# One of eight slots of each attention group read on TensorE from the table in SBUF, and the attention products in four column tiles

## The chip, the cores and the metric

The program runs on one core of one Trainium2 chip. The metric is the device time of one execution, in microseconds (us). PE is the matrix engine, DVE the vector engine, ACT the activation engine, POOL the engine that issues the gathers here, and SP issues the other DMAs.

## What is computed

A graph network on 3125 nodes (32 numbers each) and 100000 edges sorted by destination: an edge MLP, two graph convolutions and three attention layers with residuals and normalisations. The attention layer, where the change is, is this, with 8 heads of 32:

```
xl = (x @ Wl).reshape(-1, H, C); xr = (x @ Wr).reshape(-1, H, C)
e = leaky_relu(xl[src] + xr[dst], 0.2)
logits = einsum('ehc,hc->eh', e, att)
m = segment_max(logits, dst)
p = exp(logits - m[dst])
alpha = p / segment_sum(p, dst)[dst]
out = segment_sum(alpha[:, :, None] * xl[src], dst).mean(axis=1) + bias
```

## The kernel before

Edges stand in 832 slots of 128 edges. A group is 8 slots (104 groups), a chunk is 8 groups (13 chunks). The node rows lie in a table, in SBUF during a layer and in DRAM: per node 32 numbers in f32 and the same in three bf16 parts. Each attention layer goes once over the 104 groups.

For every group, POOL gathers the source rows with eight indirect DMAs (`pool_gathers`, L340), one for each slot, into one of two buffers, so it is at most two groups ahead. ACT copies the f32 part to `xs` (`keep`, L562). PE turns the source rows and reads the destination rows out of four windows (`rows_in`, L833 and L836: 48 matmuls of 128 columns, each in one of four 32-column tiles of the array), ACT copies the result (`turn`, L566), PE forms the 256 edge features in two halves (`z_half`, L848), ACT takes the relu (`leaky`, L573), and PE sums them to logits (`linear`, L856, and `logits_half`, L865, once for each half, in two column tiles). The logits of eight groups gather in one PSUM bank.

At a chunk's end (phases 0, 1 and 2 of the next chunk) DVE scans the logits for the maximum by destination (L1445, L1449). In phase 0 four transposes (L905) and `exchange` on one partition carry it over the pieces; in phase 1 `settle` subtracts it, ACT takes the exponential (L606) and PE turns the weights (L911); in phase 2 `fscale` follows a small product (L894) and scales one window of `acc`. Ten groups later (`LAG`) DVE multiplies `xs` by the weights (`weigh`, L1432, two halves), PE sums over edges (`sums_half`, L877, two halves of eight instructions), and DVE adds the sums to `acc` (`add`, L1442).

PE's order in step u, written out by hand, is: `z_half(u, 0)`, `sums_half(k, 0)`, `linear(u)`, `z_half(u, 1)`, `logits_half(u, 0)`, `rows_in(u + 1)`, `sums_half(k, 1)`, `logits_half(u, 1)`, with k = u - 10. DVE's is `weigh`, `add`, `weigh`, `add`. Semaphores join the engines, and each engine takes its instructions in this order.

Before each layer DVE makes the table, PE forms 25 windows of self logits (L947), DVE reads them (L1040, L1539), reduces them in one instruction (L1542), and clears `acc` (L1548). The convolutions already read some slots from the table in SBUF: DVE makes one-hot matrices with `is_equal` (L1304), PE multiplies them with the table (L761, 12 matmuls for one slot), DVE masks the result (L1309).

## Time and profile before

| | |
|---|---|
| median of 3 runs | 6472.8 us (6467.22 to 6487.99) |
| the profiled execution, its own time | 6470.45 us |
| its span, first to last instruction | 6468.7 us |
| PE, PE weight loads | 84%, 55% of the span |
| POOL, DVE, ACT | 65%, 50%, 30% |
| the chain that ended last | PE 40%, POOL 29%, issue 15%, DVE 9% |
| the three attention layers | from about 2734 us to 6468 us |

A line of the profile names the engine, the line of the program, the operation, what it writes and reads, and its count. "issue" is time in which the engine waited for nothing that the profile shows. Weight loads overlap the matmuls. An f32 matmul stands as two instructions. Matmuls are pipelined, so the step from one line's start to the next line's start, not the duration, is what a group of them costs.

### The profile page before, as it was taken

What the parts mean: (1) busy time and instruction counts of PE and PEld (TensorE: products, weight loads), DVE (VectorE), ACT (ScalarE), POOL (GpSimd) and SP (SyncE); (2) the same over time, 40 slices, a digit from 0 to 9 for tenths busy, and PEclk for the clock granted to TensorE, in tenths of its full rate; (3) what the DMA queues carried; (4) which work ended last, traced back from release to release, by engine and by line L of the source; (5) the groups of instructions that cost most, each with busy time, mean ns of one, the idle gap of its engine ahead of it and who ended that gap; (6) DMA issues with size and microseconds to landing.
All of it is one profiled execution on the core that took longest, in us unless ns stands there. A gap on an engine that the chain in (4) does not pass through costs nothing.

```text
span 6468.7 us, 138175 instructions
## 1 busy us (share of the span) xinstructions
PE 5462.8 (84%) x47565; PEld 3535.7 (55%) x47565; DVE 3216.3 (50%) x5767; ACT 1959.8 (30%) x3916; POOL 4227.3 (65%) x4383
## 2 busy tenths in 40 slices
PE   1888888868886888689999986899999679999995
PEld 1666666667775777535455544354444444455553
DVE  8222323266567555535555555355555624555555
ACT  0333334345551000033333321333333123333330
POOL 0777777657775777477777742777777147777770
PEclk8899989879997999789999996999999879999997
DMA  1444444323332332234444431444444224444441
GB/s 36 113 114 113 113 113 113 102 72 83 78 83 66 83 83 77 54 87 119 117 121 121 120 94 38 104 120 117 121 121 118 65 56 116 120 119 121 119 117 32
DMA packets 645340, 626.97 MB, mean 97 GB/s; under 512 B 366244, under 2 KB 447915, under 8 KB 644779
## 3 DMA queue, kind: packets, MB, share of 16 engines
q1 hardware_dynamic: 498218, 437.16, 22.1%
q0 software_dynamic: 140352, 181.29, 14.6%
q8 instruction: 312, 5.11, 0.3%
q10 hardware_dynamic: 6208, 1.37, 0.1%
q14 instruction: 250, 2.04, 0.1%
HBM read 530.77 MB, written 88.55 MB: 96 GB/s over the span
## 4 chain that ended last, share of the span: by engine, by line
PE 40%; POOL 29%; issue 15%; DVE 9%; ACT 2%; DMA 2%; DVEq 1%; POOLq 0%
POOL rows L340 29%; PE ps L761 11%; PE ps L877 10%; PE ps L848 4%; PE ps L776 4%; PE ps L865 2%; PE ps L856 2%; DMA rows<-table,idx 2%; DVE region L1326 1%; DVE acc L1442 1%; PE ps L947 1%; PE ps L833 1%; PE ps L788 1%; DVE region L1034 1%; PE ps L963 1%
## 5 line engine op out<-in xcount | busy, mean ns | idle before, releaser
L340 POOL DMA_INDIRECT rows<-table,idx x3328 | 3231.9, 971 | 1556.8 <-issue 1108.3
L877 PE MATMUL ps<-region,hot 128*128 128x272 f32 x4992 | 1320.0, 408 | 92.2 <-DVE acc L1442 87.9
L877 PEld LDWEIGHTS ps<-region,hot 128*128 128x128 f32 x4992 | 910.9, 192 | 507.9 <-issue 335.8
L573 ACT ACTIVATE region<-ps 128x512 f32<-128x512 f32 x1248 | 677.4, 595 | 1681.9 <-PE ps L848 1681.9
L1442 DVE TENSOR_TENSOR acc<-acc,ps 128x272 f32 x1248 | 545.2, 437 | 1195.6 <-PE ps L877 1088.5
L1432 DVE TENSOR_TENSOR region<-ps,region 128x1056 f32<-128x1056 f32 x624 | 781.7, 1253 | 64.8 <-issue 53.7
L761 PE MATMUL ps<-hot,region 128*128 128x192 bf16 (+1 forms) x7488 | 773.0, 266 | 13.2 <-issue 9.6
L848 PE MATMUL ps<-xT,wcat 64*128 64x512 f32 x2496 | 721.9, 655 | 7.4 <-ACT region L573 4.9
L761 PEld LDWEIGHTS ps<-hot,region 128*128 128x128 bf16 x7488 | 701.9, 105 | 40.8 <-issue 9.9
L352 POOL DMA_INDIRECT rows<-table,idx x528 | 502.6, 952 | 270.5 <-issue 160.3
L865 PE MATMUL ps<-region,attblk 128*32 128x512 f32 x2496 | 667.5, 614 | 0.0
L352 POOL DMA_INDIRECT region<-table,idx x512 | 487.2, 952 | 156.0 <-issue 156.0
L848 PEld LDWEIGHTS ps<-xT,wcat 64*128 64x128 f32 x2496 | 193.4, 189 | 463.8 <-issue 431.0
L1289 DVE TENSOR_TENSOR acc<-acc,ps 128x96 f32 (+1 forms) x832 | 252.2, 303 | 354.4 <-PE ps L788 127.5
L833 PEld LDWEIGHTS ps<-identb,rows 128*32 128x32 bf16 x7488 | 239.8, 97 | 270.5 <-issue 264.5
L833 PE MATMUL ps<-identb,rows 128*32 128x128 bf16 x7488 | 300.0, 223 | 93.1 <-DMA rows<-table,idx 89.4
L620 ACT ACTIVATE region<-iota,region 128x128 bf16<-128x128 f32 x832 | 254.2, 389 | 283.3 <-PE ps L796 270.9
L856 PE MATMUL ps<-xT,linblk 128*128 128x512 f32 x624 | 331.3, 613 | 0.0
L836 PE MATMUL ps<-turned,xwin 128*32 128x128 bf16 x7488 | 313.2, 223 | 0.0
L1231 DVE TENSOR_TENSOR region<-ps,b3row 128x512 f32<-128x512 f32 x104 | 71.9, 691 | 483.5 <-PE ps L725 483.5
L776 PE MATMUL ps<-region 128*128 128x224 f32 x1248 | 308.3, 371 | 0.0
L1309 DVE TENSOR_TENSOR region<-ps,gmask 128x448 f32<-128x448 f32 x312 | 193.8, 621 | 176.8 <-PE ps L761 176.0
(264 smaller groups left out, 5880.0 us busy)
## 6 DMA issues: line engine op xcount, KB each, us to landing
hot<-hot_dram SPq DMA_DIRECT2D x624, 256.0 KB
turned<-turned_dram SPq DMA_DIRECT2D x624, 128.0 KB
rows<-table,idx POOLq DMA_INDIRECT x3856
hot_dram<-hot SPq DMA_DIRECT2D x104, 512.0 KB
xwin<-table SPq DMA_DIRECT2D x1664, 24.0 KB
region<-hot_dram SPq DMA_DIRECT2D x78, 512.0 KB
turned_dram<-turned SPq DMA_DIRECT2D x104, 256.0 KB
region<-r_dram SPq DMA_DIRECT2D x78, 256.0 KB
```

Source lines behind the costliest of these rows:

```text
L340: pool.indirect_dma_start(rows[:, b, j, :], None, table, bass.IndirectOffsetOnAxis(ap=idx[:, s:s + 1], axis=0)).then_inc(gathered[b], 16)
L352: pool.indirect_dma_start(rows4[at % 4][:, j, :], None, table, bass.IndirectOffsetOnAxis(ap=idx[:, 8 * g + j:8 * g + j + 1], axis=0)).then ...
L573: act.activation(rz[:, 2 * t + side, :], ps[:, Z + side, :], ACT.Relu).then_inc(rz_made, 1)
L761: mm = pe.matmul(ps[:, GB + i % 2, 224 * j:224 * j + n], bt[b][:, k, at:at + P], tabparts[:, k::FOLD, (2 + s) * C:(3 + s) * C], start=(k = ...
L776: mm = pe.matmul(ps[:, DB[i % 2], 0:GROUPS * C], dhot[b][:, at, :], picked[b][:, at, :, :].rearrange("p g c -> p (g c)"), start=(j == 0), ...
L833: m1 = pe.matmul(ps[q:q + C, XT, j * P:(j + 1) * P], rowparts[b][:, at, 2 * C + s * C:2 * C + (s + 1) * C], identb[:, :], start=(s == 0), ...
L848: pe.matmul(ps[:, Z + side, :], wcat[l][q:q + 64, side, t * P:(t + 1) * P], xT[q:q + 64, g % 2, :], start=True, stop=True).then_inc(z_summ ...
L856: pe.matmul(ps[:, LG, :], linblk[l][:, (7 - n) * H:(7 - n) * H + P], xT[:, g % 2, :], start=(n == 0), stop=False, skip_group_check=True)
L865: pe.matmul(ps[q:q + 32, LG, :], attblk[l][:, t, p_:p_ + 4 * H], rz[:, 2 * t + side, :], start=False, stop=(n % 4 == 3 and t == 1), skip_g ...
L877: mm = pe.matmul(ps[:, AG + i, 0:PC + H], hot[:, b, 4 * side + 2 * i + j, :], px[b][:, 4 * side + 2 * i + j, :], start=(j == 0), stop=(j = ...
L1432: v.tensor_tensor(to, at.unsqueeze(3).broadcast_to([P, 4, H, HK]), xs[:, (k // 8) % 2, n, 4 * side:4 * side + 4, :].unsqueeze(2).broadcast ...
L1442: v.tensor_tensor(at, at, ps[:, AG + i, 0:PC + H], ALU.add).then_inc(att_added, 1)
```

## The change

In the attention layers the eighth slot of each group is no longer gathered: POOL issues seven indirect DMAs. In its place, two groups ahead, `read_one` multiplies a one-hot matrix with the table in SBUF (12 bf16 matmuls into the free columns of the first sum bank), and DVE's `pick_one` masks out the right 32 of 224 columns and sums them into `xs`. `rows_in` turns that slot with one f32 matmul in place of three bf16 ones, and waits for it. The one-hot matrices come once a chunk from four `is_equal` of 128x1024 (`stationary_one`), whose row numbers SP fetches with a broadcast DMA of 128 x 8 pieces of 256 bytes. A contiguous bf16 copy of the table (`tabC`) is made at each layer's start. There the reduction L1542 becomes seven smaller ones inside the loop over windows, and the first `pick_one` stands behind the clearing of `acc`.

The two `logits_half` become one `logits` at the end of the step: four products in four column tiles, where each half had two in two. For this the order of logits in the bank is changed from (piece, head) to (head, piece), with which the copies and views of `exchange`, `weigh`, `fall` and `fdiag` change, and two copies of `exchange` become four.

```diff
-                slots = range(8 * g, 8 * g + 8) if pas == 0 else piece_slots(g)
+                slots = range(8 * g, 8 * g + 8) if pas == 0 else piece_slots(g)[0:7]
...
+            def numbers_for(c):
...
+                if at >= 2:
+                    sp.wait_ge(bt1_made, FOLD * (at - 1))
+                first = CHUNK * c + CHUNK // 2 + PIECE - 1
+                sp.dma_start(rline1[at % 2].rearrange("p (n e) -> p n e", n=8),
+                             r_dram.rearrange("a (f e) -> (a f) e", f=2)[first:first + 29:4, :].partition_broadcast(P)
+                             ).then_inc(r1_in[at % 2], 16)
...
+                pe.wait_ge(one_kept, l * G + g + 1)
                 for j in range(4):
                     for s in range(3):
                         for side in range(2):
                             q, at = 64 * side, 4 * side + j
...
+                            elif s == 0:
+                                m3 = pe.matmul(ps[q:q + C, XT, j * P:(j + 1) * P], xs[:, (g // 8) % 2, g % 8, 7, 0:C],
+                                               ident[:, :], start=True, stop=True)
+                                m3.then_inc(x_made, 1)
...
-            def logits_half(g, t):
+            def logits(g):
                 n = g % 8
-                pe.wait_ge(rz_made, 4 * (l * G + g) + 2 * t + 2)
+                pe.wait_ge(rz_made, 4 * (l * G + g) + 4)
                 for side in range(2):
...
+                    for t in range(2):
+                        q = 64 * side + 32 * t
+                        pe.matmul(ps[q:q + 32, LG, :], attblk[l][:, t, 7 - n:7 - n + 32], rz[:, 2 * t + side, :],
+                                  start=False, stop=(n == 7), skip_group_check=True).then_inc(l_summed, 1)
+
+            def read_one(g):
...
+                for k in range(FOLD):
+                    cols = len(range(k, W, FOLD)) * C
+                    for s in range(3):
+                        mm = pe.matmul(ps[:, AG, 272:272 + cols], bt1[at % 2][:, k, n, :],
+                                       tabC[:, k::FOLD, s * C:(s + 1) * C], start=(k == 0 and s == 0),
+                                       stop=(k == FOLD - 1 and s == 2), skip_group_check=True)
+                mm.then_inc(one_read, 1)
...
+                if side == 1 or k + LAG + 2 >= G:
+                    pe.wait_ge(one_picked, l * G + min(k + LAG + 3, G))
...
+            read_one(0)
             rows_in(0)
+            read_one(1)
...
                 if u < G:
                     z_half(u, 0)
+                if u + 2 < G:
+                    if k > 0:
+                        pe.wait_ge(att_added, 4 * (l * G + k))
+                    read_one(u + 2)
...
-                    logits_half(u, 0)
...
-                    logits_half(u, 1)
+                    logits(u)
...
+            def pick_one(l, g):
...
+                v.tensor_tensor(cand, ps[:, AG, 272:272 + GROUPS * C].rearrange("p (g c) -> p g c", g=GROUPS),
+                                wide(spanhot[:, g, :], C), ALU.mult).then_inc(one_picked, 1)
+                v.wait_ge(one_picked, at + 1)
+                v.tensor_reduce(xs[:, (g // 8) % 2, g % 8, 7, 0:C], cand.rearrange("p g c -> p c g"), AX.X, ALU.add
+                                ).then_inc(one_kept, 1)
...
+                v.tensor_copy(tabC, tabparts[:, :, 2 * C:5 * C]).then_inc(tab_kept, 1)
+                attention_begins(l)
...
+                    if w % 4 == 3 or w == W - 1:
+                        lo = w - w % 4
+                        link(v.tensor_reduce(selfsum[:, lo:w + 1, :].rearrange("p w h -> p (w h)"),
+                                             prodself[:, 0:w + 1 - lo, :].rearrange("p w (h c) -> p (w h) c", h=H),
+                                             AX.X, ALU.add))
```

In DVE's step `pick_one(u + 2)` stands between `add(k, 0)` and the second `weigh`; in phases 3 and 4 two `stationary_one` each stand ahead of the first `weigh`. In `rows_in` the fourth slot of the second side is the one that is read.

## Rows read from the trace of the kernel before

**Rows 1.** Windows of 150 us inside the first attention layer: us, busy by engine, clock.
```profile
3300.00:3450.00 150.00, 146.76 (x1251) 75.33 (x1252) 79.96 (x127) 50.68 (x110) 112.41 (x118) 1.00 0.46 118
```
**Rows 2.** Timeline of POOL, first gathers: start, us, line, [idle before <- released by].
```profile
2740.07 0.94 POOL L340 DMA_INDIRECT rows<-table,idx  x1 [57.88 <-DMA table<-hot]
2741.32 0.94 POOL L340 DMA_INDIRECT rows<-table,idx  x1 [0.30 <-issue]
```
**Rows 3.** Line L856 (two per group): groups 0 to 10, then 10 to 103.
```profile
L856 PE MATMUL ps<-xT,linblk x22: 592/697/1222, 2769.1 to 2868.5; 128*128 128x512 f32 x22
...
L856 PE MATMUL ps<-xT,linblk x188: 592/593/697, 2868.1 to 3819.1; 128*128 128x512 f32 x188
```
**Rows 4.** Timeline of PE over one ordinary group, merged by line.
```profile
3302.80 2.10 PE L877 MATMUL ps<-region,hot 128*128 128x272 f32 x8
3304.83 1.05 PE L865 MATMUL ps<-region,attblk 128*32 128x512 f32 x4
3305.81 1.13 PE L848 MATMUL ps<-xT,wcat 64*128 64x512 f32 x4
3306.87 2.10 PE L877 MATMUL ps<-region,hot 128*128 128x272 f32 x8
3308.81 1.02 PE L856 MATMUL ps<-xT,linblk 128*128 128x512 f32 x2
3309.76 1.13 PE L848 MATMUL ps<-xT,wcat 64*128 64x512 f32 x4
3310.82 0.62 PE L865 MATMUL ps<-region,attblk 128*32 128x512 f32 x2
...
3312.47 2.10 PE L877 MATMUL ps<-region,hot 128*128 128x272 f32 x8
```
**Rows 5.** Timeline of PE in a convolution: the same table read, two slots.
```profile
1403.35 2.22 PE L761 MATMUL ps<-hot,region 128*128 128x224 bf16 x24
1405.41 0.95 PE L776 MATMUL ps<-region 128*128 128x224 f32 x4
```
**Rows 6.** Timeline of PE: the 48 transposes of one group by themselves, and what follows.
```profile
3260.00 0.23 PE L836 MATMUL ps<-turned,xwin 128*32 128x128 bf16 x1
...
3260.78 0.27 PE L905 MATMUL ps<-ident,region 128*1 128x128 f32 x1
```
**Rows 7.** Timeline of PE in the groups after a chunk's end.
```profile
3271.76 0.66 PE L911 MATMUL ps<-ident,region 128*128 128x128 f32 x4
...
3278.96 0.38 PE L894 MATMUL ps<-fdiag,ones 8*128 8x8 f32 x2
...
3283.48 2.07 PE L877 MATMUL ps<-region,hot 128*128 128x272 f32 x8 [0.35 <-DVE acc L1442]
```
**Rows 8.** Timeline of ACT in the same groups: the exponential.
```profile
3271.08 0.63 ACT L606 ACTIVATE region<-region 128x512 f32<-128x512 f32 x1
```
**Rows 9.** Timeline of DVE in the same groups.
```profile
3261.41 0.41 DVE L1043 COPY ahead<-ps 1x256 f32<-1x256 f32 x1 [1.94 <-PE ps L905]
...
3279.39 0.23 DVE L1037 TENSOR_SCALAR fscale<-ps,first_hot 128x8 f32<-128x8 f32 x1 [3.11 <-PE ps L894]
...
3282.90 0.44 DVE L1442 TENSOR_TENSOR acc<-acc,ps 128x272 f32 x1 [0.36 <-DVE acc L1442]
```
**Rows 10.** DVE by line and shape: count | busy us, mean ns | idle before.
```profile
L1304 DVE TENSOR_SCALAR region<-region,lanes 128x1024 bf16<-128x1024 f16 x312 | 158.1, 508 | 2.9
...
L1289 DVE TENSOR_TENSOR acc<-acc,ps 128x224 f32 x312 | 120.4, 386 | 108.5 <-PE ps L776 104.5 <-issue 1.0 <-DVE acc L1289 0.7
```
**Rows 11.** Timeline of DVE and PE at the first layer's start.
```profile
2764.71 6.81 DVE L1542 TENSOR_REDUCE hot<-region 128x200 f32<-128x6400 f32 x1
...
2773.51 5.72 DVE L1548 MEMSET acc<- 128x6800 f32 x1 [1.59 <-issue]
...
2764.85 0.29 PE L833 MATMUL ps<-identb,rows 128*32 128x128 bf16 x1 [0.72 <-DVE lself L1539]
```
**Rows 12.** The page's DMA issues: count, KB each, us from issue to landing.
```profile
table<-hot SPq DMA_DIRECT2D x6, 1000.0 KB, 5.8
```

More of the change, by code:

```diff
@@ L146, in build @@
         lane = sb("lane", [P, 1])
-        fall = sb("fall", [H, 1])
-        fdiag = sb("fdiag", [H, H])
+        fall = sb("fall", [8 * H, 1])
+        fdiag = sb("fdiag", [8 * H, H])
+        headsel = sb("headsel", [8 * H, H])
+        spanhot = sb("spanhot", [P, G, GROUPS], BF16)
         fscale = sb("fscale", [P, H])
@@ L276, in build @@
         r_made, r_stored = sem("r_made"), sem("r_stored")
+        r1_in = [sem(f"r1_in{b}") for b in range(2)]
+        bt1_made, one_read, one_picked, one_kept = sem("bt1_made"), sem("one_read"), sem("one_picked"), sem("one_kept")
+        tab_kept = sem("tab_kept")
         r_in = [sem(f"r_in{b}") for b in range(2)]
@@ L560, in keep @@
             def keep(g):
-                act.wait_ge(gathered[g % 2], 128 * ((1 + l) * HALF + g // 2 + 1))
-                act.activation(xs[:, (g // 8) % 2, g % 8, :, 0:C], rows[:, g % 2, :, 0:C], ACT.Copy).then_inc(xs_kept, 1)
+                act.wait_ge(gathered[g % 2], 128 * HALF + 112 * (l * HALF + g // 2 + 1))
+                act.activation(xs[:, (g // 8) % 2, g % 8, 0:7, 0:C], rows[:, g % 2, 0:7, 0:C], ACT.Copy).then_inc(xs_kept, 1)
             def turn(g):
@@ L893, in pe_attention @@
                     pe.wait_ge(endmax_copied, at + 1)
-                    pe.matmul(ps[:, MISC, 0:H], ones[0:H, :], fdiag[:, :], start=True, stop=True).then_inc(fall_spread, 1)
+                    pe.matmul(ps[:, MISC, 0:H], ones[0:8 * H, :], fdiag[:, :], start=True, stop=True).then_inc(fall_spread, 1)
                 if u < G:
@@ L1207, in _ @@
             cp(grp, slint)
+            ones_of = grp.rearrange("p (c a n j) -> p c a n j", c=CHUNKS, a=2, n=8)[:, :, 1, :, PIECE - 1]
+            for c in range(CHUNKS):
+                tt(spanhot[:, 8 * c:8 * c + 8, :], wide(ones_of[:, c, :], GROUPS), down(iota[:, 0:GROUPS], 8), ALU.is_equal)
             for k in range(FOLD):
@@ L1415, in _, with stationary_one, attention_begins @@
             cp(X0[:, :, :], X[:, :, :])
+            selfsum = T1[:, :, :].rearrange("p w c -> p (w c)")[:, 512:512 + W * H].rearrange("p (w h) -> p w h", w=W)
+            def stationary_one(l, c, k):
+                at = l * CHUNKS + c
+                if k == 0:
+                    v.wait_ge(r1_in[at % 2], 16 * (at // 2 + 1))
+                    if at >= 2:
+                        v.wait_ge(one_read, l * G + 8 * (c - 1))
+                v.tensor_scalar(bt1[at % 2][:, k, :, :].rearrange("p n e -> p (n e)"), rline1[at % 2], lanes[:, k:k + 1],
+                                None, ALU.is_equal).then_inc(bt1_made, 1)
+            def pick_one(l, g):
+                at = l * G + g
+                v.wait_ge(one_read, at + 1)
+                if at > 0:
+                    v.wait_ge(one_kept, at)
+                v.tensor_tensor(cand, ps[:, AG, 272:272 + GROUPS * C].rearrange("p (g c) -> p g c", g=GROUPS),
[3 more added lines that the diff above has]
+                                ).then_inc(one_kept, 1)
+            def attention_begins(l):
+                for k in range(FOLD):
+                    stationary_one(l, 0, k)
             def attention(l):
@@ L1455, in exchange @@
                     v.wait_ge(tails_turned, 4 * at + 4)
-                    got = ps[0:1, MISC, :].rearrange("p (s k r h) -> p s k h r", s=2, k=2, r=PIECES)
-                    cp(ahead[:, :, :, 1:PIECES + 1], got[:, 0, :, :, :])
-                    cp(behind[:, :, :, 0:PIECES], got[:, 1, :, :, :])
+                    got = ps[0:1, MISC, :].rearrange("p (s k a h n) -> p s a k h n", s=2, k=2, a=2, h=H)
+                    for a in range(2):
+                        cp(ahead[:, :, :, 1 + 8 * a:9 + 8 * a], got[:, 0, a, :, :, :])
+                        cp(behind[:, :, :, 8 * a:8 + 8 * a], got[:, 1, a, :, :, :])
                     lines = [t.rearrange("p h r -> p (h r)") for t in (ahead[:, 0, :, :], ahead[:, 1, :, :],
@@ L1482, in settle @@
                                            ALU.is_lt, ALU.mult).then_inc(lasts_made, 1)
-                    tt(fall[:, :], carrycol[0:H, 0:1], most_[0:H, 0:1], ALU.subtract)
-                    v.tensor_scalar(fall[:, :], fall[:, :], 0.0, first_old[0:H, c:c + 1], ALU.min, ALU.mult).then_inc(e_made, 1)
-                for u in range(8, G + LAG):
+                    tt(fall[:, :], carrycol[0:8 * H, 0:1], most_[0:8 * H, 0:1], ALU.subtract)
+                    v.tensor_scalar(fall[:, :], fall[:, :], 0.0, first_old[0:8 * H, c:c + 1], ALU.min, ALU.mult).then_inc(e_made, 1)
+                pick_one(l, 0)
+                pick_one(l, 1)
+                for u in range(G + LAG):
                     phase, c, k = u % 8, u // 8 - 1, u - LAG
@@ L1498, in attention, with pick @@
                         link(v.tensor_tensor(at, at, fscale[:, :].unsqueeze(2).broadcast_to([P, H, HK]), ALU.mult))
+                    def pick():
+                        if u + 2 < G:
+                            pick_one(l, u + 2)
+                    if phase in (3, 4) and u // 8 + 1 < CHUNKS:
+                        for q in range(2):
+                            stationary_one(l, u // 8 + 1, 2 * (phase - 3) + q)
                     if phase == 0 and ends:
@@ L1506, in attention @@
                             add(k, 0, windows)
+                        pick()
                         if 0 <= k + 1 < G:
@@ L1526, in attention @@
                             add(k, 0, windows)
+                        pick()
                         if 0 <= k + 1 < G:
```

81 lines of the change are left out of this document (49 added, 32 removed).

## The prediction

> **What bounds the kernel now.** I read the busy shares by window first. Inside an attention layer PE is busy 146.8 of 150 us at the full clock of 2.4 GHz (granted 1.00), DVE 80.0, ACT 50.7, POOL 112.4 [rows 1]. POOL's share misleads: between two gathers lie 0.30 us of issue, so one gather costs 1.25 us from start to start [rows 2], eight cost 10.0 and the 64 of a chunk 80.0. PE's ordinary group runs from L877 at 3302.80 to L877 at 3312.47, 9.67 us [rows 4]. The layer's pace, from the starts of L856 for groups 10 to 103, is (3819.1 - 0.4 - 2868.1) / 93 = 10.22 us, 81.8 a chunk (0.4 is the second instruction of the last pair) [rows 3]; the other two layers repeat it. So PE and the gathers are nearly level. A chunk is 8 x 9.67 = 77.4 of ordinary PE work, and the other 4.4 are work and waits at the chunk's end and waits for gathered rows. Two pieces are otherwise bound: in the first ten groups no edge sums run yet, and they take 99 us, the gathers' ten times 10.0 [rows 3]; at a layer's start PE waits for DVE [rows 11].
>
> **The change part by part: one group on PE.** The steps between starts [rows 4] are: z_half 1.06 twice, first sums 1.94, linear 0.95, logits_half with rows_in 1.65, second sums 2.04, last logits_half 0.98.
>
> Added: read_one is twelve matmuls. In the convolution 24 of them take 2.06 (1403.35 to 1405.41) [rows 5], so 1.03. It is in the same full-array tiling as the sums behind it, so no new switch.
>
> Removed: rows_in alone takes 0.78 [rows 6], so the first logits_half had 1.65 - 0.78 = 0.87 of the step. The last one stays at 0.98 if its eight instructions in four column tiles run together as its four in two tiles do. That is not shown for f32. The nearest row is rows_in itself, 48 matmuls of 128 columns in 0.78, which is four tiles streaming at once (48 x 128 columns at 2.4 GHz one after another would be 2.56 us). I take 0.98; the other end is one pair after the other, 0.87 more.
>
> Changed: rows_in has an f32 matmul for three bf16 ones. By its twelve per tile the pitch is about 0.06; f32 takes four passes for three, so 0.83 (between 0.78 and 1.0).
>
> Sum: 1.06 + 1.03 + 1.94 + 0.95 + 1.06 + 0.83 + 2.04 + 0.98 = 9.89, or 0.22 more than 9.67, and 1.8 a chunk.
>
> **The chunk's end.** Phase 1: the weights' transposes (L911, 3271.76) start as ACT's exponential ends (3271.08 + 0.63 = 3271.71) [rows 7, 8]; the exponential stands behind the relu of the second z_half, which doesn't move. What hid it was a logits_half and rows_in. With the first logits_half gone PE arrives 0.82 earlier and waits: 0.8 is given back.
>
> Phase 2: the second sums (3283.48) start as the second add ends (3282.90 + 0.44) [rows 7, 9], after the chain L894 (3278.96), fscale (3279.39), scaling, weigh, add. The sums now also wait for the multiply of pick_one behind that add. Its nearest row is a DVE operation of 224 columns with a PSUM operand, 0.39 [rows 10]. PE arrives 0.82 earlier, the release comes 0.33 later: 1.15. Queued behind PE's wait are the sums, the logits and all of the next group. In ordinary groups the pick has nearly 3 us of linear, z_half and rows_in as cover and costs nothing; if that cover failed it would be up to 0.9 a group.
>
> Phase 0: exchange copies 256 numbers of one partition in 0.41 [rows 9], twice; halves in four copies I estimate at 0.29 each, 0.3 more on the path to the carry (bounds 0 and 0.8). The four is_equal of 0.51 [rows 10] a chunk fall in phases 3 and 4, where DVE has idle time: 0.
>
> **The other waits.** read_one waits for the adds of the group before, a wait that the first sums had and that now comes 1.03 earlier; in ordinary groups logits and z_half, 2.04 [rows 4], lie between the sums and it, and an add is 0.44 [rows 9], so 0. Behind it stand both sums. rows_in waits for the pick of the step before: 0. SP's queue gets one more DMA a chunk and a wait for is_equal made a chunk earlier; behind it stand the loads of windows and of one-hot matrices, which run two groups ahead: 0, and at most the DMA's own time, 5.8 [rows 12], once a chunk if that lead were gone.
>
> **The gathers.** Seven cost 8.75 a group, 70 a chunk, and wait for nothing that PE then waits for. What PE waits for them now is between 0 and 81.8 - 80.0 = 1.8 a chunk; I take back 1.0. So a gain of 10 us on POOL is worth 1 us here, because PE's order is next at once.
>
> Per chunk: 1.8 + 0.8 + 1.15 + 0.3 - 1.0 = +3.05. Times 93 / 8 = 11.6 chunks and three layers: +106 us.
>
> **The first ten groups** follow the gathers: nine groups at 1.25 less are -11.2; PE's chain at the first chunk's end (scan, exchange, settle) holds some back, so -9, three times: -27 (bounds -34 and -15).
>
> **A layer's start.** rows_in(0) started at 2764.85, released by DVE's last read of a window [rows 11]. Now it needs pick_one(0), which stands behind the clearing of acc. First, DVE must have its row numbers before the windows: their DMA goes out once the table has landed (2740.07 is that landing [rows 2]), 256 KB in 1024 pieces, at least a fraction of, at most about, the 5.8 of the table's 1000 KB [rows 12]; then four is_equal, 2.0 [rows 10]. Some of that DVE had idle; I take a delay of 4 (0 to 8). The seven reductions hold the loop 1 longer. Behind it come a last small reduction and an add, 0.8; then what stands now between the add's end (2764.71 + 6.81 + 0.4) and the end of L1548 (2773.51 + 5.72), 7.3 [rows 11]; then pick_one, 0.9. Together 14, three times: +42 (bounds 27 and 57). The old reduction of 6.81 was behind PE's start and is worth nothing there. POOL's third group waits for rows_in(0), so it moves too.
>
> **Before the layers** DVE makes 13 comparisons and splits 8 flag copies into 16, all on one chain: between 0.2 and 0.39 each [rows 10], +4. No cover.
>
> Sum: 106 - 27 + 42 + 4 = +125. Against the profiled execution's 6470.45 that is 6595; that execution is 2.4 us under the median, so nothing is corrected for.
>
> On the four tiles a rule of the skill speaks against the count. The Trainium skill, "TensorE: Matmul & The Clock Gate", section "Measured speedup vs the span model", gives 2.38 times for three column tiles and 3.07 times for four row tiles of 512 columns. By 3.07 the logits would take an estimated 1.11 where I take 0.98, and the sum would be 41 us more. No row of this trace has four f32 tiles.
>
> **The rivals.** (1) The column tiles do not run together in f32: the array takes one pair, then the other, and the removed logits_half comes back behind the second sums, where it covers none of the new waits: 0.87 x 312 = +271, 6866. For: no row shows four f32 streams. Against: four bf16 streams run [rows 6].
>
> (2) No new waits: DVE and ACT shift ahead with PE so the 0.8 and 1.15 vanish, and the DMA of row numbers is covered. Then -1.95 x 34.9 = -68 and -12: 6515. For: idle time of DVE. Against: in both places PE starts within 0.15 us of the end of the work that releases it [rows 7 to 9].
>
> (3) Faster: the layer really follows gathers. Mechanism: most of the chunk's 4.4 us above 77.4 are late gathers and their echo in the waits at the chunk's end. Its place is rows_in; its price is the share that goes. Rival 2's chunk is 81.8 + 2.1 - 1.0; it decides from the point where more than 2.1 of the 4.4 are gathers' doing. With 3.4 of them gone a chunk is 1.3 shorter, -45; with -34 in the first groups, +30 at the starts and +4: 6425. For: POOL is 29% of the chain that ended last, and PE and POOL are level. Against: 81.8 - 80.0 bounds the share at 1.8, unless echoes count.
>
> (4) The pick is late in ordinary groups too (0.3 or more a group): 6690 and up.
>
> **How the numbers follow.** Forecast 0.60 (6545 to 6650 by the bounds of its terms), (1) 0.09, (2) 0.14, (3) 0.08, (4) 0.09. The range is 6480 to 6710: it takes in (2), the forecast and the lower half of (4), and leaves out (1) and (3). Within 0.3% (19 us, about what a measurement of this kernel can tell from no change) is the lower end of (2) and the upper of (3), 0.09; faster by more 0.07; slower by more 0.84.
>
> **What would show it.** The step from L856 to the next in ordinary groups: 9.9, not 9.67. The logits: 0.98 to 1.1 for eight instructions; 1.85 is rival 1. A wait of 1 us before the weights' transposes and of 1.6 before the second sums of phase 2; none there is rival 2. PE's waits for gathered rows gone inside a layer, and gaps of POOL of 1 us and more for every group. rows_in(0) some 39 us after the table's landing in place of 25. The first ten groups in about 90. The prediction is wrong if the ordinary step is under 9.7, or if the waits at the chunk's end were the gathers' echo.

## The result, and the profile after

The changed kernel takes 6550.64 us (median of 4 runs, 6542.4 to 6556.77), the kernel before on the same chip 6470.52 (4 runs): ratio 1.0117, 95% interval 1.0096 to 1.0139. It is slower, by 80 us (1.2%); forecast were 6595 and a range of 6480 to 6710. The profiled execution has 6542.4 us of its own, a span of 6540.7 and a granted clock of 0.924. The two profiled executions differ by 72 us, and the readings below add up to that.

The window of [rows 1] (us, busy by engine, clock):

```profile
3300.00:3450.00 150.00, 146.33 (x1358) 84.28 (x1350) 92.22 (x158) 47.49 (x105) 97.63 (x103) 1.00 0.47 122
```

The line of the linear product (two instructions a group) over the two stretches of [rows 3]:

```profile
L888 PE MATMUL ps<-xT,linblk x22: 592/607/1114, 2782.9 to 2873.5; 128*128 128x512 f32 x22
...
L888 PE MATMUL ps<-xT,linblk x188: 592/592/697, 2873.0 to 3846.5; 128*128 128x512 f32 x188
```

The timeline of POOL at its first gather in the layers, beside [rows 2]:

```profile
2741.29 0.94 POOL L350 DMA_INDIRECT rows<-table,idx  x1 [58.09 <-DMA table<-hot]
```

PE is as full as it was (146.3 of 150 us at full clock, before 146.8), DVE has 12 us more, POOL 15 less. The first ten groups take 90.1 us in place of 99.0 [rows 3]; from there the pace is (3846.5 - 0.4 - 2873.0) / 93 = 10.46 us a group in place of 10.22.

One ordinary group on PE, merged by line, beside [rows 4] (start, us, line, shapes):

```profile
3327.29 2.10 PE L926 MATMUL ps<-region,hot 128*128 128x272 f32 x8
3329.32 1.06 PE L897 MATMUL ps<-region,attblk 128*32 128x512 f32 x8
3330.32 1.13 PE L880 MATMUL ps<-xT,wcat 64*128 64x512 f32 x4
3331.38 1.21 PE L910 MATMUL ps<-region 128*128 128x224 bf16 x12
3332.42 2.03 PE L926 MATMUL ps<-region,hot 128*128 128x272 f32 x8
3334.29 1.02 PE L888 MATMUL ps<-xT,linblk 128*128 128x512 f32 x2
3335.24 1.13 PE L880 MATMUL ps<-xT,wcat 64*128 64x512 f32 x4
...
3337.13 2.10 PE L926 MATMUL ps<-region,hot 128*128 128x272 f32 x8
```

The step is 3337.13 - 3327.29 = 9.84 (9.67 before). By starts: sums 2.03, the eight logits 1.00 (L897), z_half 1.06, the read 1.04 (L910), sums 1.87, linear 0.95, and 1.89 for z_half with rows_in.

The timeline of PE in the groups at a chunk's end, beside [rows 7]:

```profile
3360.53 0.28 PE L975 MATMUL ps<-ident,staterow 1*128 1x1 f32 x2 [0.31 <-DVEq L1560]
3362.20 1.21 PE L910 MATMUL ps<-region 128*128 128x224 bf16 x12 [0.33 <-DVE acc L1530]
3368.91 0.66 PE L966 MATMUL ps<-ident,region 128*128 128x128 f32 x4 [0.90 <-ACT region L631]
3381.80 2.07 PE L926 MATMUL ps<-region,hot 128*128 128x272 f32 x8 [1.49 <-DVE region L1495]
```

The timeline of DVE in the same groups, beside [rows 9]:

```profile
3357.43 0.28 DVE L1098 COPY ahead<-ps 1x128 f32<-1x128 f32 x1 [0.53 <-PE ps L960]
3381.27 0.38 DVE L1495 TENSOR_TENSOR region<-ps,spanhot 128x224 f32<-128x224 f32 x1
```

And that of ACT, beside [rows 8]:

```profile
3368.23 0.63 ACT L631 ACTIVATE region<-region 128x512 f32<-128x512 f32 x1
```

Two waits of PE are new in size: 0.90 before the weights' transposes, ended by ACT's exponential, and 1.49 before the second sums, ended by the first instruction of `pick_one` (L1495). Before they were 0.05 and 0.35. The third, 0.33 before the read for DVE's add, only moved: before, the first sums of this group waited for that add, in the same timeline of the kernel before:

```profile
3266.05 2.07 PE L877 MATMUL ps<-region,hot 128*128 128x272 f32 x8 [0.41 <-DVE acc L1442]
```

The timeline of DVE at the first layer's start, beside [rows 11]:

```profile
2744.46 1.70 DVE L1486 TENSOR_SCALAR region<-T,lanes 128x1024 bf16<-128x1024 f16 x4 [7.62 <-DMA T<-r_dram]
2769.93 5.72 DVE L1653 MEMSET acc<- 128x6800 f32 x1 [1.62 <-issue]
2776.04 0.39 DVE L1495 TENSOR_TENSOR region<-ps,spanhot 128x224 f32<-128x224 f32 x1
```

And PE's rows_in(0):

```profile
2777.14 0.27 PE L860 MATMUL ps<-identb,rows 128*32 128x128 bf16 x1 [7.32 <-DVE region L1498]
```

rows_in(0) starts at 2777.14 where it started at 2764.85, and the 7.32 us ahead of it are a wait for the pick behind the clearing of `acc`.

The waits between 3000 and 3800 us (us in total, times, longest):

```profile
POOL rows L350 <- ACT region L587: 137.5, 66, 4.7
PE ps L926 <- DVE region L1495: 13.8, 9, 1.8
PE ps L966 <- ACT region L631: 9.0, 10, 0.9
```

POOL now has idle time in nearly every group (66 waits, 2.1 us on average); PE waits for the pick once a chunk and in no ordinary group.

Where the 72 us are, from the starts of the linear product and of rows_in in all three layers:

| stretch | forecast | measured |
|---|---|---|
| up to the first table store | +4 | +1.2 |
| three layer starts | +42 | +36.7 |
| three times groups 0 to 10 | -27 | -21.7 |
| three times groups 10 to 103 | +106 | +57.3 |
| the rest | 0 | -1.5 |

The first four experiments ran on one chip, with the kernel before at 6471.23 us (one of its 13 executions there took 21197.4 us and is left out of the ratios); that is within 1 us of the 6470.52 beside the changed kernel, so their times are set beside its 6550.64. The others ran on two further chips, on which the kernel before itself took 8225.59 and 8211.69 us, so their ratios to it are what can be compared; where two times are given, they are from these two chips in this order. The changed kernel itself was run on neither.

### The profile page after: what moved, and what is told of

The parts are those of the page before. It is cut to its first block, busy times and chain, and to the rows that moved or that the text cites. A ratio compares the mean times of both kernels' runs of the same rounds, so it can differ in the third digit from the quotient of the medians.

```text
span 6540.7 us, 146855 instructions
## 1 busy us (share of the span) xinstructions
PE 5464.1 (84%) x50997; PEld 3747.4 (57%) x50997; DVE 3552.2 (54%) x6668; ACT 1937.5 (30%) x3916; POOL 3931.6 (60%) x4071
## 4 chain that ended last, share of the span: by engine, by line
PE 61%; POOL 15%; DVE 10%; issue 10%; ACT 2%; DVEq 1%; DMA 1%; POOLq 0%
PE ps L926 18%; POOL rows L350 15%; PE ps L786 11%; PE ps L880 8%; PE ps L910 5%; PE ps L897 4%; PE ps L801 4%; PE ps L888 3%; PE ps L860 2%; DVE region L1386 1%; PE ps L813 1%; DVE acc L1530 1%; DVE region L1089 1%; PE ps L1018 1%; ACT region L598 1%
## 5 line engine op out<-in xcount | busy, mean ns | idle before, releaser
L350 POOL DMA_INDIRECT rows<-table,idx x3016 | 2936.8, 974 | 1927.3 <-issue 962.5
L926 PE MATMUL ps<-region,hot 128*128 128x272 f32 x4992 | 1299.1, 404 | 114.5 <-DVE region L1495 49.7
L362 POOL DMA_INDIRECT rows<-table,idx x528 | 502.8, 952 | 264.6 <-issue 160.3
L910 PEld LDWEIGHTS ps<-region 128*128 128x128 bf16 x3744 | 310.4, 99 | 262.3 <-issue 213.3
L910 PE MATMUL ps<-region 128*128 128x192 bf16 (+1 forms) x3744 | 382.6, 253 | 18.1 <-DVE acc L1530 12.2
L860 PEld LDWEIGHTS ps<-identb,rows 128*32 128x32 bf16 x6552 | 212.8, 97 | 300.8 <-issue 300.8
L897 PE MATMUL ps<-region,attblk 128*32 128x512 f32 x2496 | 343.5, 621 | 2.6 <-ACT region L598 2.6
L860 PE MATMUL ps<-identb,rows 128*32 128x128 bf16 x6552 | 267.5, 222 | 64.7 <-DMA rows<-table,idx 42.7
```

The lines of the kernel that those rows point to most:

```text
L350: pool.indirect_dma_start(rows[:, b, j, :], None, table, bass.IndirectOffsetOnAxis(ap=idx[:, s:s + 1], axis=0)).then_inc(gathered[b], 16)
L362: pool.indirect_dma_start(rows4[at % 4][:, j, :], None, table, bass.IndirectOffsetOnAxis(ap=idx[:, 8 * g + j:8 * g + j + 1], axis=0)).then ...
L860: m1 = pe.matmul(ps[q:q + C, XT, j * P:(j + 1) * P], rowparts[b][:, at, 2 * C + s * C:2 * C + (s + 1) * C], identb[:, :], start=(s == 0), ...
L897: pe.matmul(ps[q:q + 32, LG, :], attblk[l][:, t, 7 - n:7 - n + 32], rz[:, 2 * t + side, :], start=False, stop=(n == 7), skip_group_check=T ...
L910: mm = pe.matmul(ps[:, AG, 272:272 + cols], bt1[at % 2][:, k, n, :], tabC[:, k::FOLD, s * C:(s + 1) * C], start=(k == 0 and s == 0), stop= ...
L926: mm = pe.matmul(ps[:, AG + i, 0:PC + H], hot[:, b, 4 * side + 2 * i + j, :], px[b][:, 4 * side + 2 * i + j, :], start=(j == 0), stop=(j = ...
```

## The experiments

The theory going in: PE's order binds the changed kernel; the chunk's two waits (exponential, pick) and the pick behind the clearing are what it lost beyond the ordinary step; the four tiles run together. The main rival: the gathers still matter, in the kernel before above all.

### The four tiles alone

The kernel before with the new logits, all eight gathers and no read.

```diff
-                    logits_half(u, 0)
...
-                    logits_half(u, 1)
+                    logits(u)
```

> The kernel before with the second half of the change alone: all eight slots are gathered, none is read from the table, and the four logits products of a group stand at the end of the step in four column tiles (with the new order of logits in the bank). Theory (PE's order sets the pace, the gathers stand just behind it): PE's ordinary group falls from 9.67 to 8.8 us, but eight gathers stay at 10.0, so the group goes to 10.0, the chunk from 82.0 to about 81, and the layers' starts stay as they were: about 6440 us, 0.3 to 0.7 per cent faster than before. Rival (waits for gathers are small and PE's work is what counts): each chunk is 5 us or more shorter, 6290 us. Rival (four f32 column tiles cost as much as two pairs): no gain, 6470 to 6500 us.

Measured: 6465.72 us (10 runs), ratio 0.9997, interval 0.9987 to 1.0007. No change. Its groups 10 to 103 of the first layer, by the line of the linear product:

```profile
L885 PE MATMUL ps<-xT,linblk x188: 592/592/698, 2871.7 to 3825.1; 128*128 128x512 f32 x188
```

Its waits between 3000 and 3800 us (us in total, times, longest):

```profile
POOL rows L350 <- issue: 193.7, 597, 2.5
POOL rows L350 <- ACT region L586: 8.5, 28, 0.3
PE ps L858 <- DMA rows<-table,idx: 49.8, 41, 2.8
```

The same waits in the kernel before:

```profile
POOL rows L340 <- issue: 198.8, 610, 3.5
POOL rows L340 <- ACT region L562: 4.9, 16, 0.3
PE ps L833 <- DMA rows<-table,idx: 6.9, 16, 1.3
```

PE's unobstructed group is 8.82 us here, 0.85 under the 9.67 of before, so it is not the rival of four tiles that cost as much as two pairs, though the time alone would fit that too. The pace is (3825.1 - 0.4 - 2871.7) / 93 = 10.25. The 0.85 went into waiting: for gathered rows the profile names 49.8 us in 800 where it named 6.9. The gathers are the reason. In both kernels POOL's mean distance from gather to gather in that window is 1.28 us, not the 1.25 of two neighbours [rows 2], and 8 x 1.28 = 10.24, the pace of both. By itself that equation says nothing, since any steady loop with eight gathers has an eighth of its pace as their mean distance. What decides is that POOL hardly waits: for a free buffer 4.9 us of 800 before and 8.5 here. The mean is 1.28 also over the second to eighth gather of every group alone, before which the program has no wait. Most of what lifts it over 1.25 is one distance of 3.0 to 4.5 us that comes in the attention layers at nearly every 112th gather (21 of 22 times in the kernel before), always the second of a group. One of them in POOL's timeline of the kernel before:

```profile
3321.67 0.94 POOL L340 DMA_INDIRECT rows<-table,idx  x1 [2.23 <-issue]
```

So the kernel before did not have the gathers near its bound: it ran at their pace. What the 112 comes from, no run shows.

### The read alone

The changed kernel with the logits back in two halves of two tiles each, at their old places.

```diff
+                    logits_half(u, 0)
                 if u + 1 < G:
                     rows_in(u + 1)
...
-                    logits(u)
+                    logits_half(u, 1)
```

> The changed kernel with the logits back in two halves at their old places, two column tiles each: the read from the table alone. Theory: PE's ordinary group is 9.83 + 0.87 = 10.7 us, 7.0 a chunk; the half ahead of rows_in covers the wait for the exponential (0.9) and part of the wait for the pick in phase 2 (0.9 of 1.5) again, so a chunk is 84.0 + 7.0 - 1.7 = 89.3 and the time 6542 + 35 x 5.3 = about 6728 us. Rival (the waits at the chunk's end are not a matter of cover): they stay, 6542 + 35 x 7.0 = 6787 us. Rival (the four tiles save less than a half): under 6680 us.

Measured: 6723.41 us, ratio 1.0382 (1.0364 to 1.0401), as the theory had it. PE in an ordinary group:

```profile
3327.97 1.05 PE L896 MATMUL ps<-region,attblk 128*32 128x512 f32 x4
3328.95 1.13 PE L880 MATMUL ps<-xT,wcat 64*128 64x512 f32 x4
```

Four instructions in two tiles take 0.98 here, eight in four tiles 1.00 in the changed kernel. The pace is 11.09 us a group. The four tiles are thus worth 6723 - 6551 = 172 us beside the read and 0 without it: the same edit, with PE's order as the bound in the one kernel and the gathers in the other.

### The exponential ahead of the relus

In phase 1 ACT takes the exponential before the relu of the second z_half, not behind it.

```diff
-                if u < G:
-                    leaky(u, 1)
                 if phase == 1 and 0 <= done < CHUNKS:
                     act.wait_ge(d_made, l * CHUNKS + done + 1)
                     act.activation(weight, weight, ACT.Exp).then_inc(weight_made, 1)
+                if u < G:
+                    leaky(u, 1)
```

> The changed kernel with one swap on ACT: in phase 1 the exponential of the weights stands ahead of the relu of the second half. Theory: PE's wait of 0.90 before the transposes of the weights goes, but the second sums behind them then wait for the pick (its multiply ends at 3368.70, the sums start at 3369.41), so 0.6 a chunk are won: -21 us, 6521 to 6530 us. Rival (that wait is an echo of DVE's chain and comes back elsewhere): no change, 6550 us. Rival (nothing is next): -31 us.

Measured: 6524.08 us, ratio 1.0076 (1.0058 to 1.0094); 26 us under the changed kernel. The line of the weights' transposes in this kernel, 3300 to 3450 us, with the idle time before it (matmuls and weight loads counted together):

```profile
L967 PE MATMUL ps<-ident,region x8: 272/273/328, 3364.0 to 3447.9; 128*128 128x128 f32 x8
...
  issue: 0.3, 2
```

The same in the changed kernel:

```profile
L966 PE MATMUL ps<-ident,region x4: 272/273/327, 3368.9 to 3369.3; 128*128 128x128 f32 x4
...
  ACT region L631: 2.0, 2
```

The wait is gone (two chunk ends in the window, 0.3 us in all). That it was this wait, in this place, is shown; it is not worth its whole 0.90. In the two profiled executions (15 us apart, where the medians are 26 apart) the group with the exponential takes 11.71 us in place of 12.19 in most chunks, 0.48 less, and the first ten groups of the three layers take 1.5, 3.7 and 1.6 us less. The next wait takes the rest, as was expected: PE's sums now wait for the pick in this group too. Between 3000 and 3800 us:

```profile
PE ps L927 <- DVE region L1496: 18.3, 20, 1.8
```

The changed kernel has 13.8 us in 9 waits there.

### The first picks ahead of the clearing

```diff
                 v.wait_ge(zn_read, (l + 1) * W)
+                pick_one(l, 0)
+                pick_one(l, 1)
                 tt(lself[:, :, :], lself[:, :, :], selfsum, ALU.add)
...
-                pick_one(l, 0)
-                pick_one(l, 1)
                 for u in range(G + LAG):
```

> The changed kernel with the first two picks of a layer ahead of the clearing of acc on DVE. Theory: rows_in(0) of each layer starts 6 us earlier (its wait for the pick is 7.3 us, of which a pick of 0.9 stays), nothing behind it is late: -18 us over three layers, 6524 to 6533 us. Rival (the first groups follow something else, such as DVE's clearing before the third pick, or the gathers): less than 6 us in all.

Measured: 6527.34 us, ratio 1.0084 (1.0066 to 1.0102); 23 us under the changed kernel. The timeline of PE at the first layer's start:

```profile
2768.55 0.27 PE L860 MATMUL ps<-identb,rows 128*32 128x128 bf16 x1 [1.24 <-DVE region L1498]
```

And of DVE:

```profile
2767.45 0.39 DVE L1495 TENSOR_TENSOR region<-ps,spanhot 128x224 f32<-128x224 f32 x1 [2.05 <-PE ps L910]
...
2775.12 5.72 DVE L1653 MEMSET acc<- 128x6800 f32 x1 [1.62 <-issue]
```

From the table's store to rows_in(0) it is now 35.4, 35.9 and 36.6 us in the three layers (changed kernel 41.9, 42.4, 42.5; before 30.8, 31.5, 31.6). So of the 11 us that a start lost, 6 to 6.5 were the place behind the clearing. Of the other 4.5 to 5 only 1.0 to 1.5 are a later end of the 25 windows (the row numbers, the four `is_equal` and the smaller reductions together: 31.9, 32.4 and 33.0 us behind the store, before 30.7, 31.4 and 31.6); the other 3.5 are the read and the pick of group 0 one after the other. In the profiled executions the whole is worth 16 us, by the medians 23. The pace inside the layer stays at 10.45.

### Eight gathers beside the read

The changed kernel with the eighth gather issued again, its rows unused; run on each of the two slower chips.

```diff
-                slots = range(8 * g, 8 * g + 8) if pas == 0 else piece_slots(g)[0:7]
+                slots = range(8 * g, 8 * g + 8) if pas == 0 else piece_slots(g)
```

> The changed kernel with POOL gathering all eight slots again (the eighth row block is gathered and not used; the slot is still read from the table). It asks what the gather taken off POOL is worth. Theory: behind PE's order of 84.0 us a chunk the 82 us of eight gathers are hidden, a few late ones show, so the chunk stays under 84.5; only the first ten groups of a layer lose their 7 us: +25 to +35 us on the changed kernel, 6575 to 6585 us. Rival (gathers set the pace too): +2 us a chunk, 6640 us or more.  Rival (the gather is worth nothing anywhere): 6550 us.

> The changed kernel with all eight gathers of a group issued, the eighth landing where nothing reads it. Theory: the gathers then need 64 x 1.28 = 82 us a chunk, TensorE 84.0; each lands late in a part of the groups, and the two wait for each other in turn: 25 to 35 us above the changed kernel, 6575 to 6585. Rival, GpSimd doesn't matter at all, since TensorE's order binds every group: 6551. Rival, the gathers bound the kernel before and the dropped one was worth its whole 8 x 1.28 = 10.2 a chunk: 84.0 becomes more than 90, 6750 and more.

Measured: 8511.62 us, ratio 1.0336 (1.0321 to 1.0352), and 8504.88, ratio 1.0352 (1.0335 to 1.0369). Without the changed kernel on these chips the price of the gather over it can't be read off, and neither theory nor rival is decided; the comparison that can be made is with the next run.

### The two edits together

The exponential ahead of the relus and the picks ahead of the clearing, seven gathers.

> The changed kernel with the exponential ahead of the relus and the first two picks ahead of clearing the sum, both together. Alone they gave 26 and 23 us. Theory: they lie in different places (the chunk's end, the layer's start), so they add: 6551 - 49 = 6502. Rival: both take from one slack (the transfers of the layer's first groups, which a late start leaves ready), 6515 to 6525.

Run on the second of the two chips. Measured: 8113.03 us, ratio 0.9879 (0.9863 to 0.9895): on this chip faster than the kernel before, by 1.2%. Neither theory had a ratio under 1, and whether the 26 and the 23 us add can't be told. Groups between 4000 and 4800 us (two instructions of the linear product each) in this kernel and, behind it, with eight gathers on the same chip, with POOL's wait for a free buffer there:

```profile
L889 PE MATMUL ps<-xT,linblk x124: 592/592/697, 4000.6 to 4791.2; 128*128 128x512 f32 x124
```

```profile
L888 PE MATMUL ps<-xT,linblk x114: 592/592/697, 4006.4 to 4798.3; 128*128 128x512 f32 x114
...
POOL rows L350 <- ACT region L587: 223.5, 53, 6.5
```

62 groups against 57: 12.9 against 14.0 us each. The exponential explains about 0.1 of the 1.1 (0.5 to 0.7 a chunk on the first chip), so the eighth gather costs about 1 us a group there, nearly its whole 1.25, on a chip where TensorE's ordinary 9.83 is no longer what sets the pace. But the gathers do not bind there as they did in the kernel before: POOL waits 4.2 us a time (223.5 / 53), nearly once a group, until ACT has copied a buffer and it is free again. That each gather lengthens this circle of gathering, copying and freeing one of two buffers fits the rows; it was not tested.

### Reading in every second group

Odd groups read, even groups gather all eight; with the two edits of the last kernel.

```diff
-                slots = range(8 * g, 8 * g + 8) if pas == 0 else piece_slots(g)[0:7]
+                slots = range(8 * g, 8 * g + 8) if pas == 0 else piece_slots(g)[0:8 - b]
...
-                if u + 2 < G:
+                if u + 2 < G and u % 2 == 1:
```

> A mixture of both kernels: one slot is read from the table in every second group only (the odd ones), eight slots are gathered in the others; four column tiles, exponential first, first pick ahead of the clearing. Theory (PE and the gathers must be balanced, and the two halves of the change need one another): PE's groups are 9.83 and 8.82 in turn, 74.6 us a chunk and some 4.4 at its end, 79.0; 60 gathers of 1.28 are 76.8; so 3 us a chunk under the kernel before, the layers' starts 4 us later: 6370 us (6350 to 6410), 1.5 per cent faster than before. Rival (the gathers with their late ones bind above 60 x 1.28): 6420 us. Rival (the read costs more than its matmuls): over 6450 us.

> The slot is read on TensorE in odd groups alone, even groups gather all eight; four column tiles; the exponential ahead of the relus; in a layer's start only the first odd pick ahead of clearing the sum. Per pair of groups: gathers 15 instead of 16, so a chunk has 60 x 1.28 (mean start to start of the gathers in before, without waits) = 76.8 us of GpSimd; TensorE 4 groups of 9.83 less the 1.04 of a read = 8.79 and 4 of 9.83 = 74.5, and 4.5 at the chunk's end (the 5.36 of after less 0.8 for the exponential) = 79.0. Theory (TensorE's order binds): 79.0 a chunk against 84.0, 5.0 x 11.6 x 3 = 174 less than the changed kernel's 6551, and 20 less at the starts: 6350 to 6410, taken 6370, 1.5% under before. Rival (gathers are late here as in the kernel with eight gathers and four tiles, where the pace stayed at 82 though TensorE's groups had 8.82): pace between 78 and 80, 6400 to 6450. A third: the group without a read leaves its pick's slot free but the group with one is as late as before, 84.0 kept: 6520.

Measured: 8252.99 us, ratio 1.0030 (1.002 to 1.004), and 8240.38, ratio 1.0033 (1.002 to 1.0045). Between 4000 and 4800 us:

```profile
L890 PE MATMUL ps<-xT,linblk x120: 592/592/697, 4003.2 to 4790.2; 128*128 128x512 f32 x120
```

60 groups, 13.3 us each, between the 12.9 of seven gathers and the 14.0 of eight. The pace here goes with the number of gathers, not with TensorE's instructions, of which this kernel has the fewest of the three. The theory, 1.5% faster than the kernel before, missed on both chips. The 6370 us were worked out for TensorE's order as the bound on a chip like the first, and that was not run: whether this version beats the kernel before there stays open.

### The pick at the start of DVE's step

So that the sums of a chunk's second step need not wait for it; the sums take their banks in the order 1, 0.

```diff
-                if side == 1 or k + LAG + 2 >= G:
-                    pe.wait_ge(one_picked, l * G + min(k + LAG + 3, G))
-                for i in range(2):
+                for i in (1, 0):
+                    if i == 0 and side == 0:
+                        pe.wait_ge(one_picked, l * G + min(k + LAG + 3, G))
```

> The changed kernel with DVE's pick at the start of its step (between or behind the scans in phases 0 and 1), and the bank that it reads written last by the sums, so that the second sums no longer wait for it. Theory: in phase 2 the second sums start behind the second add (0.44 earlier at most, since the add ends 0.38 before the pick's multiply), nothing else moves: -12 to -15 us, 6536 us. Rival (the pick is the whole wait of 1.49): -50 us. Rival (the wait of the first sums for the pick costs 0.1 or more in ordinary groups): slower than the changed kernel.

> The changed kernel with VectorE's pick at the start of its step, so that sums behind it never wait for it at the end of a chunk; the sums of a group then take their two banks in the order 1, 0, and the first product of bank 0 waits for the pick. Theory (the pick in the chunk's second step, late by 1.49, is what it costs): 13.8 us of such waits in 800 are gone, some 5450/800... taken over the three layers' 3800 us at most 4.5 x 13.8 = 62, of which the weighing behind the pick gives back 0.92 in many steps: 6500 to 6540. Rival: the pick now waits in VectorE's queue for the read of its own step, and the weighing and the adds stand behind it, so TensorE's sums wait for VectorE's and the other way round: each group longer by 0.5 to 1.5, 6700 to 7000.

Measured: 9011.58 us, ratio 1.0951 (1.0923 to 1.098), and 8983.6, ratio 1.0937 (1.0907 to 1.0967). Eight gathers beside the read have 1.0336 and 1.0352, so it is likely slower than the changed kernel too, which was not run there. The theory fell, and the rival's mechanism is in the trace; its size on the first chip is open. Waits between 4000 and 4800 us, on the second chip:

```profile
DVE region L1495 <- remote: 229.8, 40, 7.9
PE ps L926 <- DVE region L1495: 63.6, 16, 4.9
```

The timeline of PE at one pair of sums:

```profile
4317.60 1.11 PE L926 MATMUL ps<-region,hot 128*128 128x272 f32 x4
4320.73 1.18 PE L926 MATMUL ps<-region,hot 128*128 128x272 f32 x4 [2.03 <-DVE region L1495]
```

The pick waits 5.7 us at a time with DVE's adds and weighing queued behind it, and the first sums of a group stop half way for the pick. The place of the pick behind the first add, as in the change, keeps the two queues apart. How much of the 9.4% this would be on the first chip was not run.

### All three together

The last edit with the exponential and the first picks moved, on the first of the two chips.

> The changed kernel with the exponential first, the first two picks ahead of the clearing, and the pick at the start of DVE's step, together. Theory (three separate waits on PE's path): 0.9 + 0.4 a chunk and 6 to 7 us a layer: -46 - 20 = -66 us, about 6484 us, still behind the kernel before by 0.2 per cent. Rival (they are one another's echo): over 6510 us. Rival (without these waits the read and the four tiles pay): under 6460 us.

Measured: 8974.28 us, ratio 1.0911 (1.0891 to 1.0931), 37 us under the pick edit alone on the same chip. So the loss of the third edit stays whole beside the other two, whose gain there is 37 together, where they gave 26 and 23 singly on the first chip.

## Why the prediction was right in sign and too high by 45 us

The range and the sign held, by the forecast's own mechanism: PE's order became the next bound. Rivals 1, 2 and 4 fell by rows above (eight logits instructions in 1.00 us; both waits there; no pick wait in ordinary groups). Rival 3 said that the layer follows the gathers, and in that it was right, as the four tiles alone showed; the prediction had put the two nearly level. Its size was wrong: chunks of the kernel before whose ordinary groups all ran at PE's 9.67, by the starts of L856, took 80.6 to 80.9 us, so taking the gathers away was worth 1.1 to 1.4 of a mean chunk of 82.0, not the 3.4 of the rival, and PE's own order was next.

**The ordinary group**, forecast 9.89, measured 9.83 to 9.84. The read (1.03, measured 1.04), the logits (0.98, measured 1.00), z_half with rows_in (1.06 + 0.83, measured 1.89) are as forecast. The term that was mis-sized is the sums behind the read, taken over from [rows 4] as 1.94 and measured at 1.87. The likely reason is that the 1.94 held a change of tiling, from z_half's 64 rows to the full array, which now stands before the read: the prediction said "no new switch" and did not take the old one out. That is argued, not shown; the read, where the change should then cost as much, took 1.04 with 1.03 forecast. It is 0.07 less of the step; eight steps give +1.28 a chunk (9.83 - 9.67 = 0.16), not +1.8.

**The chunk's end**, forecast 0.8 + 1.15 + 0.3 = 2.25. A chunk of the changed kernel repeats at 84.0 = 8 x 9.83 + 5.36; one of before without late rows has 80.6 to 80.9, 3.2 to 3.5 over 77.4. The difference is 1.9 to 2.2, close to the forecast, and term by term it is right. In the cleanest chunks the three groups at the chunk's end took 10.67, 11.34 and 10.18 before and take 11.16, 12.19 and 11.47 now. Less the 0.16 of the ordinary step these are +0.33 for exchange (forecast 0.3: its four copies take 0.28 each, and PE now waits 0.31 for it at L975), +0.69 for the exponential (0.8) and +1.13 for the pick (1.15). The wait of the read for the adds, forecast at 0, is 0.33 once a chunk, and took the place of the 0.41 that the first sums had waited.

**The gathers**, forecast -1.0 a chunk, measured -1.1 to -1.4 (82.0 less 80.9 or 80.6). The picture behind it was wrong: the prediction counted a gather at 1.25 and so 80.0 a chunk, with 1.8 of air. The mean is 1.28 and the air is none, as the four tiles alone showed. It cost nothing here, because PE's order without late rows is only 1.1 to 1.4 below the gathers. That the size came out near is in part luck. A forecast of the four tiles alone by the same picture was 6440, and 6466 came out.

Together +2.0 for a full chunk (84.0 against 82.0); over groups 10 to 103 the mean is 57.3 / (11.6 x 3) = +1.64, since that stretch holds 11 chunk ends and not 11.6, and its last two groups read nothing (8.86 each). Forecast +3.05, times 11.6: the ordinary step and the gathers are about 0.9 of the 1.05 that a chunk came out lower.

**The first ten groups**, forecast -27, measured -21.7: 98.9, 97.9 and 97.6 us became 90.2, 92.4 and 90.1. The 9 in place of 11.2 that PE's chain was to hold back was still too much, by 1.8 a layer. With the exponential ahead of the relus these groups take 88.5 to 88.8, so part of what held them back was the same wait.

**The layer's start**, forecast 14 each, measured 11.1 + 1.5, 10.9 + 1.2 and 10.9 + 1.2 (to rows_in(0), and from there to the first linear product), 12.2 on average. The term that was mis-sized is the delay of the windows, 4 for the row numbers and 1 for the reductions: the row numbers land 3.4 us after their DMA (2741.05 to 2744.46) and the four `is_equal` take 1.70, but the 25 windows end only 1.4 to 1.6 us later than before (32.3, 32.8 and 33.0 us behind the store), since before, too, DVE read its first window only 9.0 us behind the store (now 10.8). The clearing with 1.62 of issue is 7.3, as forecast; moving the picks ahead of it gave back 6 of 11. The 1.2 to 1.5 behind rows_in(0) were not in the forecast: the read of group 1 (about 1.03) now stands there.

**Before the layers**, forecast +4, measured +1.2.

**The four tiles.** The logits took 1.00 us where the forecast had 0.98. The Trainium skill, "TensorE: Matmul & The Clock Gate", section "Measured speedup vs the span model", would have made it an estimated 1.11 and the sum 41 us more; the trace does not agree, eight instructions in four f32 tiles take what four take in two.

**What stays open.** On the two slower chips a group needs 12.9 to 16 us, though with eight gathers beside the read 26 groups still ran at PE's unobstructed 9.83. Which of SP's loads, the gathers' landing and the engines' late instructions (below) makes the rest was not separated. The changed kernel was not run on these chips, nor reading in every second group on a chip like the first.

## What to carry to other kernels

Where two engines are level, an edit that lightens one gives nothing by itself and the same edit gives its full worth once the other has been lightened: the four tiles were worth 0 us alone and 172 beside the read. Take the pace of a train of DMAs from its mean over several hundred of them, not from two neighbours, and only where their issuer waits for nothing (here the second to eighth gather of a group); compare it with the loop's pace before calling anything air. When matmuls are taken out of an order written by hand, look up what stood behind each of them on the other engines: in the chunk's end two waits grew by 2.0 us, more than the 1.3 that its eight ordinary steps gained, and half of one of them went with an exchange of two instructions on ScalarE.

## What was not expected of the hardware

Four f32 products of 512 columns (eight instructions) in four column tiles take 1.00 us, two (four instructions) in two tiles 0.98, and one on the full array 0.95: four f32 streams run side by side with almost no loss. The sums take 1.94 us behind 64-row matmuls and 1.87 behind full-array ones; 0.07 is then the most that a change of tiling cost there.

An indirect DMA every 1.25 us on GpSimd is 1.28 on average. In the attention layers nearly every 112th comes 3.0 to 4.5 us behind the one before it, and nothing is shown as waited for; with seven gathers a group it is the 112th too (18 of 19 times).

On the slower chips the engines paused inside runs of instructions that wait for no semaphore. SP's instructions on the line that loads the windows, with eight gathers beside the read on such a chip (4000 to 4800 us; durations min/median/max in ns), and then in the changed kernel on the first chip (3000 to 3800 us):

```profile
L400 SPq ALU_OP  x397: 3/34/712, 4003.0 to 4799.8; - x199
L400 SPq MOVE xwin<-table x226: 2/14/1275, 4003.2 to 4798.4; - x113
```

```profile
L400 SPq ALU_OP  x532: 32/37/45, 3002.7 to 3795.2; - x178
L400 SPq MOVE xwin<-table x304: 29/29/29, 3002.9 to 3795.4; - x152
```

A register operation that takes 37 ns takes up to 712, and a move of 29 up to 1275, though the medians are no longer than on the first chip. PE's weight loads show the same in the middle of the 48 transposes of a group (the two edits together):

```profile
4315.57 0.09 PEld L868 LDWEIGHTS ps<-turned,xwin 128*32 128x32 bf16 x1
4316.96 0.09 PEld L861 LDWEIGHTS ps<-identb,rows 128*32 128x32 bf16 x1 [1.30 <-issue]
```

TensorE's products themselves are not slower: with eight gathers the granted clock is 0.88 from 4000 to 4400 us, but every linear product there takes 592 to 697 ns, as on the first chip, so the lower clock does not show in them. Instructions that arrive late would look like this; no experiment here took that apart, so it is an argument and not shown.
